# Score products over 48 and 50 rows in place of 126 and 128, and no zeros in the queries

## The reference

```python
Q = jnp.einsum('bsd,hkd->bhsk', x, WQ)
K = jnp.einsum('bsd,hkd->bhsk', x, WK)
V = jnp.einsum('bsd,hkd->bhsk', x, WV)
scores = jnp.einsum('bhqd,bhkd->bhqk', Q, K) / math.sqrt(d_k)
scores = jnp.where(causal, scores, -jnp.inf)
probs = jax.nn.softmax(scores, axis=-1)
attn = jnp.einsum('bhqk,bhkv->bhqv', probs, V)
return jnp.einsum('bhsv,hdv->bsd', attn, WO)
```

## Time and profile before

| | us |
|---|---|
| median of 3 runs | 408.97 |
| lowest, highest | 408.82, 411.0 |
| the profiled execution | 409.43 |
| its span, first to last instruction | 407.7 |

### The profile page before, as it was taken

The page is one execution under the profiler, slowest core; times in us unless marked ns, Lnnn a source line. Parts: engine busy times, 40 slices in busy tenths (PEclk is TensorE's granted clock), DMA queues, the critical chain, the costliest instruction groups (busy, mean ns, idle before and its releaser), DMA issues.

```text
span 407.7 us, 11164 instructions
## 1 busy us (share of the span) xinstructions
PE 330.6 (81%) x3642; PEld 265.4 (65%) x3642; DVE 327.9 (80%) x1215; ACT 236.9 (58%) x574; POOL 239.6 (59%) x321
## 2 busy tenths in 40 slices
PE   2447979999999999999999998988415999899940
PEld 1225667776776777776777776755314999899930
DVE  7846789969889889898898898777660999899980
ACT  2202567576576675684774864655204788788940
POOL 4831364565385585674664766558360388788883
PEclk9998999999999999999999999999555999999985
DMA  7563574664553544625535537012036667767600
GB/s 219 109 114 52 91 171 89 90 121 89 82 104 74 91 94 53 114 75 73 110 71 80 116 71 102 21 41 67 16 95 161 180 174 189 201 171 196 193 30 6
DMA packets 34680, 42.78 MB, mean 105 GB/s; under 512 B 5465, under 2 KB 25053, under 8 KB 33088
## 3 DMA queue, kind: packets, MB, share of 16 engines
q1 hardware_dynamic: 31744, 37.43, 45.0%
q0 software_dynamic: 2304, 4.37, 3.2%
q10 hardware_dynamic: 576, 0.27, 0.3%
HBM read 30.59 MB, written 11.66 MB: 104 GB/s over the span
## 4 chain that ended last, share of the span: by engine, by line
PE 42%; DVE 17%; issue 11%; DMA 11%; ACT 9%; POOL 8%; SPq 1%; POOLq 0%; DVEq 0%; ACTq 0%
PE O L871 6%; PE S L837 5%; PE ST L850 3%; DMA aug<-nmT 3%; DVE nmf L1113 3%; PE S L832 3%; PE MB L797 3%; ACT p L609 3%; POOL out_x L540 3%; PE O L875 2%; DMA w1s<-in_w1x 2%; DMA aug<-qk_parts 2%; PE MB L885 2%; POOL xs_rows L473 2%; ACT xn L659 2%
## 5 line engine op out<-in xcount | busy, mean ns | idle before, releaser
L1113 DVE TENSOR_REDUCE nmf<-S 128x2 f32<-128x512 f32 (+1 forms) x192 | 129.6, 682 | 33.9 <-PE S L837 25.5
L609 ACT ACTIVATE p<-ST 128x1024 f32<-128x1024 f32 x64 | 65.5, 1023 | 30.6 <-PE ST L850 30.5
L453 POOL TENSOR_SCALAR_AFFINE_SELECT p<-p 128x512 f32<-128x512 f32 x64 | 40.7, 636 | 52.6 <-ACT p L613 52.0
L449 POOL TENSOR_SCALAR_AFFINE_SELECT p<-p 128x512 f32<-128x512 f32 x64 | 40.5, 633 | 31.1 <-ACT p L609 30.8
L837 PE MATMUL S<-aug 126*128 126x128 bf16 x512 | 50.7, 221 | 0.0
L540 POOL DMA_INDIRECT out_x<-vaug,x_all x39 | 42.4, 1087 | 7.9 <-issue 7.9
L837 PEld LDWEIGHTS S<-aug 126*128 126x128 bf16 x512 | 40.3, 99 | 3.7
L832 PE MATMUL S<-causal,identb 128*128 128x256 bf16 x128 | 35.9, 281 | 7.6 <-DVE nmf L1113 7.2
L850 PE MATMUL ST<-aug 128*128 128x256 bf16 x256 | 38.5, 272 | 3.9 <-DMA aug<-nmT 2.6
L871 PE MATMUL O<-p,vaug 128*32 128x256 f32 x512 | 41.1, 390 | 0.5 <-POOL p L449 0.5
L613 ACT ACTIVATE p<-ST 128x512 f32<-128x512 f32 x64 | 38.8, 606 | 0.0
(11 more groups left out here) (162 smaller groups left out, 862.2 us busy)
## 6 DMA issues: line engine op xcount, KB each, us to landing
w1s<-in_w1x SPq DMA_DIRECT2D x39, 259.0 KB, 3.2
qk_parts<-qkp SPq DMA_DIRECT2D x16, 384.0 KB, 3.3
aug<-qk_parts SPq DMA_DIRECT2D x32, 192.0 KB
aug<-qk_parts SPq DMA_DIRECT2D x32, 128.0 KB
x_all<-xs_rows SPq DMA_DIRECT2D x39, 67.0 KB, 2.2
aug<-qk_parts SPq DMA_DIRECT2D x32, 64.0 KB
w_tab<-in_w2t SPq DMA_DIRECT2D x8, 256.0 KB
out_x<-vaug,x_all POOLq DMA_INDIRECT x39, 3.0
```

Of the source, the lines that this page charges most:

```text
L449: g.affine_select(out=v, in_=v, compare_op=ALU.is_ge, fill=0.0, base=0, pattern=[[0, 4], [1, P]], channel_multiplier=-1).then_inc(s["sel0" ...
L453: g.affine_select(out=v, in_=v, compare_op=ALU.is_ge, fill=0.0, base=0, pattern=[[0, 4], [1, P]], channel_multiplier=-1).then_inc(s["sel1" ...
L609: a.activation(p0[:, gr % 2], ST0[:, :, :], ACT.Exp, scale=SCALE).then_inc(s["exp0"], 1)
L1113: v.tensor_reduce(dst, S[:, n % 2].rearrange("p (j n) -> p j n", j=k), op=ALU.max, axis=AX_X, negate=True).then_inc(s["red"], 1)
```

## The change

The two rows of maxima move from rows 126 and 127 to rows 48 and 49. The products of `scores_by_query` contract rows 0 to 47, and those of `scores_near` and `scores_far` rows 0 to 49. The three memsets of `qaug`, their semaphore and the two waits for it go. The keys' memsets stay, since rows 48 and 49 of `kaug` must be ones. `MATMUL`, `LDWEIGHTS` and DMA counts are the same; `P` is 128, `DH` is 8, so `SHIFT` is 48 and `DEEP` is 50.

```diff
-    SHIFT = P - 2
+    SHIFT = 6 * DH
+    DEEP = SHIFT + 2
...
-                sp.dma_start(qaug[SHIFT:P, p, 8 * half:8 * half + 8].rearrange("c h (q t) -> c (h q) t", t=P),
+                sp.dma_start(qaug[SHIFT:DEEP, p, 8 * half:8 * half + 8].rearrange("c h (q t) -> c (h q) t", t=P),
...
-            sp.wait_ge(s["qzero"], 1)
...
-            sp.wait_ge(s["qzero"], 3)
...
-                    last = mm(ST0[:, j], kaug[:, p, h, 0:P], qaug[:, p, h], start=True, stop=True)
+                    last = mm(ST0[:, j], kaug[0:DEEP, p, h, 0:P], qaug[0:DEEP, p, h], start=True, stop=True)
...
-                    last = mm(ST1[:, j], kaug[:, p, h, P:SEQ], qaug[:, p, h, P:SEQ], start=True, stop=True)
+                    last = mm(ST1[:, j], kaug[0:DEEP, p, h, P:SEQ], qaug[0:DEEP, p, h, P:SEQ], start=True, stop=True)
...
-            v.memset(qaug[:, 0].bitcast(F32), 0.0).then_inc(s["qzero"], 1)
...
-            v.memset(qaug[:, 1].bitcast(F32), 0.0).then_inc(s["qzero"], 1)
-            v.memset(qaug[:, 2].bitcast(F32), 0.0).then_inc(s["qzero"], 1)
```

More of the change, by code:

```diff
@@ L207, in sandwich_kernel @@
         MB = ps("MB", [P, 512])
-        names = ("w_attn w_cent w_ffn x_in x_next x_rest qzero kone ids_r consts pmem vmem vones "
+        names = ("w_attn w_cent w_ffn x_in x_next x_rest kone ids_r consts pmem vmem vones "
                  "st_x agg_x ve_x rs_x nb_x xn_r xnT_r xnT_d qk_r hi_d r1_d mid_d parts_d "
```

## The result

The changed kernel takes 460.49 us (median of 4 executions, 449.88 to 476.39) against 409.86 us before (median of 4, 408.82 to 411.0). The ratio is 1.10, 95% interval 1.0944 to 1.1056: slower. The ratio compares the executions near each kernel's shortest, here 449.88 and 450.91 us, which lie in my range of 420 to 456, while the two longer ones (470.07, 476.39) and with them the median lie above it. The profiled execution took 450.91 us with a span of 449.2, so it stands 41.5 us above the span before. I had said 436.

A forecast was written before the change was run, and what follows sets the result against it. PE was taken to set the attention loop's pace: 14.6 us work, 2.5 new passages and 0.4 waits make a 17.5 us step. All terms add 26.5 us to 409.4, giving 435.9, stated as 436; range 420 to 456.

The forecast's parts named there:

- The passage: Switching PE between 128-row and few-row products costs 0.092 us each way; 27 new per attention-loop step, 2.5 us a step.
- steps 3 to 14: Twelve steady steps of the attention loop, each 17.5 us, 1.7 more than now: +20.4 us together.
- batch 0: Batch 0 alone, 25.60 to 38.10 us, before the steady loop: 22 new passages, +0.8 us, between 0 and 2.0.
- step 0: First step of the attention loop: the wait for the shift's DMA takes most of the 2.5 us, leaving +0.8.
- steps 1 and 2: Early attention-loop steps with little waiting to hide new passages: +4.0 us together.
- the last step: Last attention-loop step, no new scores by query: 11 new passages, bound by chains of old batches, +0.5 us.
- The products and the zeros: Score products over fewer rows gain 0; removing the memsets at the start gives back 0 to 0.1 us, taken as 0.
- A: Rival: the array passes between row counts without running empty; only the zeros' 0 to 0.1 us remain, 409.3 us; chance 0.12.
- B: Rival: freed DVE time at the start or sooner-ending few-row products make it faster, 406.5 us; chance 0.03.
- C: Rival: few-row weights not loaded ahead or fast, 2.6 to 3.5 us a step on top, some 480 us; chance 0.03.
- D: Rival: PE, empty more often, has its clock fall to 1.2 GHz inside the loop, 440 to 600 us; chance 0.02.
- Step 0's cover: In the first attention-loop step, the 2.0 us wait for the shift's DMA would hide most of 2.5 us of passages.

## Why the prediction was right, and where its sum was not

**The passage: right.** 0.092 us was read from the 32-column form, and the row forms cost 0.093 to 0.106: L831 to L836 0.210 instead of 0.109, L826 to L829 0.322 instead of 0.216, L849 to L826 0.093 more. The 27 new ones, less the 0.8 us of waits that take them in, gave 17.5; the step is 17.55. Two small errors cancel in this: at about 0.10 us each the passages cost 2.7 and not 2.5 (an estimate from the distances above), and the waits took in about 1.0. Over steps 3 to 14 this made +21.3 us against the forecast +20.4. Counted from the weight loads in the trace, new passages are 27 in each of these steps as I had it, 22 in batch 0, 21 in step 0, 25 in steps 1 and 2 and 8, not 11, in the last step.

**The products and the zeros: right.** L836 among themselves start 0.055 apart over 48 rows as over 126. The zeros gave nothing: DVE waits for x and for ACT where the memsets were.

**Rivals.** A (rows don't count) fell with the pair of 62 and 66 rows. The border lies between 64 and 66 rows: the change from 128 to 126 rows, which I took as speaking for it, stays inside one form. B (faster) found no time. C (loads no longer hidden within a group) fell with the 0.055.

**What failed: "PE would still issue most of the time, which speaks against it" under D.** I tied the clock to how much time PE spends issuing. The products of 48 rows in the two kernels with added products have no gap between them, and the clock stayed at 1.2 GHz in one and fell to it in the other. In the changed kernel this isn't seen where I looked for it: among the 128-row products inside the loop the clock stays up in most steps, and the profiled execution shows one fall there, too short for a 5 in the clock's row. The loss sits at both ends: the clock rises at 58.4 instead of 28.7 and falls 9 us earlier into the last step. So the terms for batch 0 (+0.8, measured 2.3), step 0 (+0.8, measured 6.0) and the last step (+0.5, measured 5.4) were mis-sized, by 11.6 of the 15 us (1.3 of these are step 0's cover, below). The last step's term would have been too large in the execution in which the clock falls 16.3 us into it: 27.65 us, less than before. That the time still fell into the range is partly luck: its upper end was worked out from dearer passages with waits kept and from a mild D, and what filled the room was the clock at both ends, which I had given a chance of 0.02; the longer executions lie outside. Beside that, were read too literally: the 0.86 for batch 0 counts the time before 28.7 us as full clock, for which there is no record, and L837 products start 0.107 us apart in it, as at 1.2 GHz.

**Step 0's cover.** I let the 2.0 us wait for the shift's DMA take most of the passages. At 1.2 GHz the products alone used it up, as the 19.78 us of the 66-row kernel show, which are full; so the passages came on top with 2.1.

**Steps 1 and 2** grew by 5.9 instead of 4.0. The clock falls once more in step 1, from 68.6 to 72.1 us. With 62 and 64 rows (the second of those executions) there is no such fall, step 1 takes 16.83 us instead of 18.25, and both steps together 33.44, 4.5 more than before. So 1.4 of the 1.9 missing are the clock again, and 0.5 the size of the term.

**What stays open.** With 62 and 64 rows the shortest executions were 442.3 and 443.9 us, with 48 and 50 rows 444.9 to 452.6, though the steady step is the same; that fits a clock that goes by rows, but with one profile for each batch of executions it is an inference. So is the step from the products without gaps to the kernel's own start. Where nothing was added at the start, the clock first rises at 38.9 us or earlier in the kernels with 126 and 128 rows and at 48.2 or later in all with fewer, but this rise differs by 10 us even where the start is the same: in the kernel before with products added behind the loop (first 48 rows) it comes at 38.9 instead of 28.7, and the first near scores then begin at 39.57 instead of 38.10. Why one execution rises at 58 us and another at 108 isn't settled either. The 66-row kernel is longer than before by 0.8% with no passages; its late clock in one profile would explain that, and only there was it seen.

## What to carry to other kernels

In these runs fewer contraction rows made no product shorter, and a product of 64 rows or fewer among products of 128 pays 0.09 to 0.11 us on the way in and again on the way out; if the contraction is to be cut, keep it above 64 rows or put the few-row products together, which no run here tried. Rows of zeros that cost nothing to stream can hold up the clock, so count the rows in use, and not only the busy time, before you take padding out. And read the clock before its first recorded change from the lengths of equal products, not from the clock's row.

## What the hardware showed that I had not expected

- Products of 48 rows without a gap left the clock at 1.2 GHz for 25.3 us, and let it fall 3.3 us after products of 126 rows had held it up; 66 rows left it there for 12.5 us; 126 rows raised it after 4.0 and 5.5 us, and 126 and 66 in turn after 5.2 (351.1 to 356.3).
- The passage costs 0.105 us at 2.4 GHz and 0.11 at 1.2, so it hardly goes with the array's clock.
- Kernels that differ only in rows show their first rise at 28.7, 30.6 and 38.9 us (126 and 128 rows, the kernel before and the two with products added behind the loop), 48.2 (48 by query, 128 for the others), 56.7 (66 and 68), 59.3 and 86.6 (62 and 64), and 58.2, 58.4 and 108.1 (48 and 50).
